# Causal attention stage: turns written out, normed tiles transposed in place, V's bias moved into one output row

## The chip, the cores and the metric

The kernel runs on one core of one Trainium2 chip. Its five engines (TensorE, shown as PE, with its weight loads as PEld; VectorE, DVE; ScalarE, ACT; GpSimd, POOL; SyncE, SP) run their own instruction streams and meet at semaphores. The metric is device time in microseconds (us) for one execution, the median of several; the profile is of one further execution.

## The reference

Two adaLN layers over x of 16 sequences of 256 tokens and 128 channels. Layer 0 has a scan mixer and a six-deep local-attention transformer, layer 1 a causal multi-query attention, then a Mamba block, then a mixture of experts. The change is in the multi-query attention of layer 1:

```python
qkv = x @ wqkv + bqkv
q = qkv[..., :DIM].reshape(b, l, HEADS, HD)       # 16 heads of 8
k = qkv[..., DIM:DIM + HD]                        # one key and one value head for all
v = qkv[..., DIM + HD:]
scores = jnp.einsum('blhd,bmd->bhlm', q, k) / np.sqrt(HD)
scores = jnp.where(causal, scores, jnp.finfo(scores.dtype).min)
attn = jax.nn.softmax(scores, axis=-1)
out = jnp.einsum('bhlm,bmd->blhd', attn, v).reshape(b, l, DIM)
return out @ w_attn_out + b_attn_out
```

Each row of `attn` sums to 1, so a bias b on V adds b to every head's output, and `tile(b, 16) @ w_attn_out` to every row of the result.

## The kernel before

`build` runs the stages one after another, each in a block that ends with a barrier: opening, transformer (six layers), `between_stage` (gate, residual, layer norm into `y`), `mqa_stage` (the stage of the change), mamba, gate, between, mixture of experts, store. In `mqa_stage` the argument `h` is `y`, which lies in SBUF as 32 tiles of 128 tokens; a sequence (a unit) is two tiles.

Work is a software pipeline over 16 units in 19 turns. In turn n, unit n has its front made (transposes L1646, products with Wq L1651 and Wk L1654), unit n-1 its scores (mask L1675, q times k L1681) and at the turn's end its values (`values`, L1657 to L1666), unit n-2 its turned scores (L1700) and first products with V (L1716), unit n-3 the rest and its output (L1737, L1738). `body` of each engine is the order written by hand, and there is no planner. `all_turns` (L1537) writes turns 0 to 3 and 16 to 18 out, with whole numbers for the unit, and runs turns 4 to 15 in a hardware loop of three rounds of four turns, where the semaphore values that are waited for come out of registers. So turn 3 is a written-out turn with all four parts in it, turns 4 to 15 are looped ones, and turn 16 is written out and lacks a front.

`values` fills V for a unit: for each of two tiles a product hT times Wv (32 columns, of which 8 are V) and a second product of a row of ones with `bv`, which adds V's bias and puts the 1 into column 8 (the softmax denominator's column). ScalarE copies both tiles (L1811) into the ring `V1`. On PE what stands behind is the mask of the next unit's first scores, which waits for `maxed`, that is for VectorE's last maximum (L1859) of the turn; the four values steps and that wait are the last thing of a turn on PE.

The transposes at L1646 read `hu`, a double buffer in SBUF that SyncE fills by DMA from `y` (`load`, L1598 to L1600), since a looped turn has no constant address into `y`. The output is added into `y` by VectorE (L1883), three turns later than the front of the same unit.

A matmul of float32 operands shows as two MATMUL records, and one transpose as one.

Of the kernel before, what the change touches and what calls it, by code (L numbers as in the profile page):

```python
# [10 lines left out]
ALU = mybir.AluOpType  # L11
ACT = mybir.ActivationFunctionType
# [4 lines left out]
P = 128  # L17
B = 16
T = 256
TT = T // P  # L20
# [4 lines left out]
class Kernel:  # L25
# [5 lines left out]
    def sb(self, ctx, name, shape, dt=F32):  # L31
        return ctx.enter_context(self.nc.sbuf_tensor(name, shape, dt))
# [5 lines left out]
def sems(nc, ctx, names):  # L38
    return [ctx.enter_context(nc.semaphore(n)) for n in names.split()]
# [1460 lines left out]
QH, QD = 16, 8  # L1500
QG, QS = 4, 4
MQ_ROUNDS = B // 4


def pairs_of_units(engine, body):

    with engine.Fori(0, B // 2 - 1) as i:
        body(i * 2, 0, True)
        body(i * 2 + 1, 1, True)
    body(B - 2, 0, True)  # L1510
    body(B - 1, 1, False)


def tile_of(h, u, t):

    if isinstance(u, int):
        return h[:, u * TT + t, :]
    return h[:, bass.ds(u * TT + t, 1), :].rearrange("p a c -> p (a c)")


class Turn:
# [11 lines left out]
    def has(self, lag):  # L1533
        return not isinstance(self.I, int) or 0 <= self.unit(lag) < B


def all_turns(engine, body):  # L1537
    for k in range(4):
        body(Turn(0, k))
    with engine.Fori(1, MQ_ROUNDS) as I:  # L1540
        for k in range(4):
            body(Turn(I, k))
    for k in range(3):
        body(Turn(MQ_ROUNDS, k))


def mqa_stage(k, h):

    nc, d = k.nc, k.dram
    SCORED = [(0, 0, 0, 4), (0, 1, 0, 4), (1, 0, 0, 2), (1, 1, 0, 2), (1, 0, 2, 2), (1, 1, 2, 2)]
    TURNED = [(0, 0, 0), (0, 0, 1), (1, 0, 0), (1, 0, 1), (1, 1, 0), (1, 1, 1)]
    with ExitStack() as ctx:
        sb = lambda name, shape, dt=F32: k.sb(ctx, "mq_" + name, shape, dt)
        Wq, Wk, Wv, Wout = sb("Wq", [P, QS, P]), sb("Wk", [P, P]), sb("Wv", [P, 32]), sb("Wout", [P, P])
        bq, bk = sb("bq", [P, QS]), sb("bk", [P, 1])
        bv, bout, ones = sb("bv", [1, 32]), sb("bout", [1, P]), sb("ones", [1, P])
        mask32 = sb("mask32", [P, 1, P])
        mask = sb("mask", [P, 1, P], BF16)  # L1560
        identb = sb("identb", [P, P], BF16)
        scratch = sb("scratch", [P, 1])
        hu = sb("hu", [P, 2, TT, P])
        hT = sb("hT", [P, 2, T])
# [3 lines left out]
        V1 = sb("V1", [P, 4, TT, 32])  # L1568
# [9 lines left out]
        ev = lambda name, n=1: Event(nc, ctx, "mq_" + name, n)  # L1578
        loaded, inited, masked = sems(nc, ctx, "mq_loaded mq_inited mq_masked")
        hu_ready = [ev("hu_ready0", 16), ev("hu_ready1", 16)]  # L1580
        f_filled, f_copied = ev("f_filled", 4), ev("f_copied", 4)
# [7 lines left out]
        @block.sync  # L1589
        def _(sp):  # L1590
            for e in hu_ready:
                e.start(sp)
            for dst, name in ((Wq[:, :, :], "mqa_Wq"), (Wk[:, :], "mqa_Wk"), (Wv[:, :], "mqa_Wv"),
                              (Wout[:, :], "L1_attn_w_attn_out"), (bq[:, :], "mqa_bq"), (bk[:, :], "mqa_bk"),
                              (bv[:, :], "mqa_bv"), (bout[:, :], "mqa_bout"), (mask32[:, :, :], "causal_mask")):
                sp.dma_start(dst, d[name]).then_inc(loaded, 16)

            def load(u, p):  # L1598
                sp.wait_ge(f_filled.sem, f_filled.at(u - 2, 1))
                sp.dma_start(hu[:, p, :, :], h[:, bass.ds(u * TT, TT), :]).then_inc(hu_ready[p].sem, 16)  # L1600

            with sp.Fori(0, B // 2) as i:
                load(i * 2, 0)
                load(i * 2 + 1, 1)

        @block.gpsimd
        def _(pool):
            nc.gpsimd.memset(mx[:, :, :, :], 0.0).then_inc(inited, 1)
            nc.gpsimd.memset(ones[:, :], 1.0).then_inc(inited, 1)
            kept.start(pool)  # L1610
            settled.start(pool)
            pool.wait_ge(loaded, 144)

            def keep(n, i, j):
                u, (t, block_, pair) = n.unit(2), TURNED[i]
                pool.wait_ge(settled.sem, settled.at(u, j))
                pool.wait_ge(exped.sem, exped.at(u, i + 1))
                nc.gpsimd.tensor_tensor(scratch[:, :], k.ident[:, 0:1], k.ident[:, 0:1], ALU.mult).then_inc(settled.sem, 1)
                heads = PT[:, i // 2, 2 * pair:2 * pair + 2, :].rearrange("p g (s c) -> p (g s) c", c=P)
                nc.gpsimd.affine_select(heads, heads, pattern=[[0, 2 * QS], [1, P]], base=0, channel_multiplier=-1,  # L1620
                                        compare_op=ALU.is_ge, fill=0.0).then_inc(kept.sem, 1)

            def body(n):
                if n.has(2):
                    keep(n, 0, 0)
                    keep(n, 1, 1)
                    keep(n, 4, 2)
                    keep(n, 5, 3)

            all_turns(pool, body)  # L1630

        @block.tensor
        def _(pe):
            for e in (f_filled, v_filled, scored, x_filled, e_filled, pv_done, back, o_turned, y_done):
                e.start(pe)
            pe.wait_ge(loaded, 144)
            pe.wait_ge(inited, 2)
            pe.wait_ge(masked, 2)

            def front(n, part):  # L1640
                u, p = n.unit(0), n.ring(0, 2)
                if part == 0:
                    pe.wait_ge(hu_ready[p].sem, hu_ready[p].at(n.I * 2 + n.k // 2, 16))
                    pe.wait_ge(v_copied.sem, v_copied.at(u - 2, 1))
                    for t in range(TT):
                        last = nc.tensor.transpose(front_ps[:, t * P:(t + 1) * P], hu[:, p, t, :], k.ident[:, :])  # L1646
                else:
                    pe.wait_ge(f_copied.sem, f_copied.at(u, part))
                    if part < 3:
                        for j in range(2):  # L1650
                            last = nc.tensor.matmul(front_ps[:, j * T:(j + 1) * T], Wq[:, 2 * part - 2 + j, :], hT[:, p, :],  # L1651
                                                    start=True, stop=True)
                    else:
                        last = nc.tensor.matmul(front_ps[:, 0:T], Wk[:, :], hT[:, p, :], start=True, stop=True)  # L1654
                last.then_inc(f_filled.sem, 1)

            def values(n):  # L1657
                u, p = n.unit(1), n.ring(1, 2)
                pe.wait_ge(v_copied.sem, v_copied.at(u - 1, 1))
                if n.has(0):  # L1660
                    pe.wait_ge(f_copied.sem, f_copied.at(n.unit(0), 4))
                for t in range(TT):
                    at = slice(t * 32, (t + 1) * 32)
                    nc.tensor.matmul(front_ps[:, at], hT[:, p, t * P:(t + 1) * P], Wv[:, :], start=True, stop=False)
                    last = nc.tensor.matmul(front_ps[:, at], ones[:, :], bv[:, :], start=False, stop=True)
                last.then_inc(v_filled.sem, 1)  # L1666
# [67 lines left out]
            def output(n, t):  # L1734
                u = n.unit(3)
                pe.wait_ge(oT_ready.sem, oT_ready.at(u, t + 1))
                nc.tensor.matmul(back_ps[:, P:2 * P], oT[:, t, :], Wout[:, :], start=True, stop=False)  # L1737
                nc.tensor.matmul(back_ps[:, P:2 * P], ones[:, :], bout[:, :], start=False, stop=True).then_inc(y_done.sem, 1)  # L1738

# [30 lines left out]

            all_turns(pe, body)

        @block.scalar
        def _(act):
            for e in (f_copied, v_copied, exped, ot_copied, oT_ready):
                e.start(act)
            act.wait_ge(loaded, 144)

            def exponential(n, i):
# [6 lines left out]
            def front(n, part):  # L1786
# [13 lines left out]
                else:  # L1800
                    if not isinstance(u, int) or u >= 4:
                        act.wait_ge(e_filled.sem, e_filled.at(u - 4, 6))
# [3 lines left out]
            def values(n):  # L1806
                u = n.unit(1)
                act.wait_ge(v_filled.sem, v_filled.at(u, 1))
                if not isinstance(u, int) or u >= 4:
                    act.wait_ge(pv_done.sem, pv_done.at(u - 4, 3))  # L1810
                nc.scalar.activation(V1[:, n.ring(1, 4), :, :], front_ps[:, 0:TT * 32].rearrange("p (t e) -> p t e", t=TT),  # L1811
                                     ACT.Copy).then_inc(v_copied.sem, 1)
# [29 lines left out]

            all_turns(act, body)

        @block.vector
        def _(dve):
# [33 lines left out]
            def add_output(n, t):  # L1880
                u = n.unit(3)
                dve.wait_ge(y_done.sem, y_done.at(u, t + 1))
                nc.vector.tensor_tensor(tile_of(h, u, t), tile_of(h, u, t), back_ps[:, P:2 * P], ALU.add)\  # L1883
                    .then_inc(y_added.sem, 1)
# [17 lines left out]

            all_turns(dve, body)

# [350 lines left out]


NE, MR, NS, MS = 16, P // 4, 2, P // 2
HID = NE * MR + NS * MS
# [345 lines left out]
```

## Time and profile before

| | us |
|---|---|
| median of 3 runs | 5036.1 (5034.69 to 5037.89) |
| the profiled execution | 5033.68 |
| its span | 5031.5 |
| multi-query attention in it | 3668.5 to about 4154 |

The page gives each engine's busy time over the span and then its share in 40 slices. The stage lies in slices 30 to 33 counted from 1. PE busy counts the modelled ends of pipelined matmuls, so full PE says that PE was never without a matmul in flight. "issue" as a releaser says that no semaphore held the engine. The mark PEclk is the granted share of TensorE's clock, 1.00 for 2.4 GHz and 0.50 for 1.2 GHz.

### The profile page before, as it was taken

What the parts mean: (1) busy time and instruction counts of PE and PEld (TensorE: products, weight loads), DVE (VectorE), ACT (ScalarE), POOL (GpSimd) and SP (SyncE); (2) the same over time, 40 slices, a digit from 0 to 9 for tenths busy, and PEclk for the clock granted to TensorE, in tenths of its full rate; (3) what the DMA queues carried; (4) which work ended last, traced back from release to release, by engine and by line L of the source; (5) the groups of instructions that cost most, each with busy time, mean ns of one, the idle gap of its engine ahead of it and who ended that gap; (6) DMA issues with size and microseconds to landing.
All of it is one profiled execution on the core that took longest, in us unless ns stands there. A gap on an engine that the chain in (4) does not pass through costs nothing. (4 is left out here: it accounts for less than half of the span.)

```text
span 5031.5 us, 167186 instructions
## 1 busy us (share of the span) xinstructions
PE 4556.1 (91%) x73156; PEld 2966.4 (59%) x73156; DVE 3206.1 (64%) x4495; ACT 2803.1 (56%) x4080; POOL 2573.5 (51%) x1408
## 2 busy tenths in 40 slices
PE   7499999999999999999999999999679998999465
PEld 5266666666666666666666666666445544555244
DVE  3476766767666767667666767677333326888554
ACT  4256665656665656666565656666433435666355
POOL 0266666666666666666666666666221114666400
PEclk8699999999999999999999999999879978999799
DMA  1100001000110010000100011000100002111100
GB/s 53 49 13 18 20 16 37 24 17 20 30 27 20 17 30 24 23 20 17 38 21 18 20 28 32 18 17 19 37 12 5 5 0 76 69 68 69 46 8 21
DMA packets 192843, 138.23 MB, mean 27 GB/s; under 512 B 122572, under 2 KB 178901, under 8 KB 190053
## 3 DMA queue, kind: packets, MB, share of 16 engines
q1 hardware_dynamic: 192101, 127.32, 8.5%
q8 instruction: 590, 9.67, 0.8%
q14 instruction: 152, 1.25, 0.1%
HBM read 68.37 MB, written 4.29 MB: 14 GB/s over the span
## 5 line engine op out<-in xcount | busy, mean ns | idle before, releaser
L1017 POOL TENSOR_TENSOR tf_qk<-tf_qk,tf_rot 128x1024 f32<-128x1024 f32 x384 | 908.7, 2366 | 1217.7 <-DVE tf_rot L1400 1217.7
L1083 PE MATMUL tf_psum<-tf_Wqkv,tf_xsT 128*128 128x512 f32 x1536 | 749.6, 611 | 68.2 <-issue 44.5
L1024 POOL TENSOR_TENSOR tf_qk<-tf_qk,tf_rn 128x1024 f32<-128x1024 f32 x384 | 724.3, 1913 | 54.3 <-ACT tf_rn L1283 54.2
L1276 ACT ACTIVATE tf_sq<-tf_psum 128x1024 f32<-128x1024 f32 x384 | 393.3, 1024 | 533.8 <-DVE tf_rot L1400 533.8
L1396 DVE TENSOR_TENSOR tf_qk<-tf_psum,tf_table 128x1024 f32<-128x1024 f32 x384 | 467.5, 1218 | 265.9 <-PE tf_psum L1083 264.8
L1156 PE MATMUL tf_psum<-tf_probT,tf_V 32*64 32x64 f32 (+1 forms) x27648 | 493.8, 219 | 8.6 <-issue 8.1
L1083 PEld LDWEIGHTS tf_psum<-tf_Wqkv,tf_xsT 128*128 128x128 f32 x1536 | 274.5, 194 | 352.4 <-issue 341.6
L1406 DVE TENSOR_REDUCE tf_ss<-tf_sq 128x16 f32<-128x1024 f32 x384 | 457.6, 1192 | 21.6 <-ACT tf_sq L1276 21.6
L1156 PEld LDWEIGHTS tf_psum<-tf_probT,tf_V 32*64 32x64 f32 x27648 | 442.8, 133 | 47.5 <-issue 42.6
L1400 DVE TENSOR_TENSOR tf_rot<-tf_psum,tf_table 128x1024 f32<-128x1024 f32 x384 | 465.9, 1213 | 0.0
L1065 PE MATMUL tf_psum<-ident,tf_qk 128*128 128x128 f32 x3072 | 408.9, 276 | 3.4 <-ACT tf_qT L1295 2.4
L1065 PEld LDWEIGHTS tf_psum<-ident,tf_qk 128*128 128x128 f32 x3072 | 343.7, 141 | 102.7 <-issue 82.1
L2013 POOL TENSOR_TENSOR mb_read<-mb_state,mb_Csb 128x1024 f32<-128x1024 f32 x128 | 301.6, 2356 | 175.1 <-DVE mb_state L2233 160.0
L1459 DVE SCALAR_TENSOR_TENSOR tf_hT<-tf_psum,tf_b,tf_gel 128x512 f32<-128x512 f32 x144 | 107.5, 746 | 438.4 <-ACT tf_gel L1328 438.4
L1179 PE MATMUL tf_psum<-tf_Wo,tf_oT 128*128 128x128 f32 x3072 | 376.3, 275 | 6.7 <-issue 3.7
L1179 PEld LDWEIGHTS tf_psum<-tf_Wo,tf_oT 128*128 128x128 f32 x3072 | 362.3, 192 | 31.9 <-issue 21.4
L1032 POOL TENSOR_TENSOR tf_prob<-tf_prob,tf_rden 128x1024 f32<-128x1024 f32 x192 | 367.2, 1912 | 13.6 <-DVE tf_rden L1430 13.6
L1099 PE MATMUL tf_psum<-tf_Wqkv,tf_xsT 128*32 128x512 f32 x3072 | 369.5, 598 | 0.0
L1295 ACT ACTIVATE tf_qT<-tf_psum 128x1024 f32<-128x1024 f32 x192 | 196.4, 1023 | 279.0 <-PE tf_psum L1065 278.9
L1124 PEld LDWEIGHTS tf_psum<-tf_kT,tf_qT 64*32 64x32 f32 x24576 | 260.6, 105 | 107.8 <-issue 107.5
L2181 ACT ACTIVATE mb_psum<-mb_delta,mb_A 128x255 f32<-128x255 f32 x512 | 213.4, 462 | 188.3 <-DVE mb_state L2233 185.8
L1124 PE MATMUL tf_psum<-tf_kT,tf_qT 64*32 64x64 f32 x24576 | 295.8, 226 | 21.0 <-issue 21.0
(288 smaller groups left out, 7907.2 us busy)
## 6 DMA issues: line engine op xcount, KB each, us to landing
mb_Csb<-mb_kept SPq DMA_DIRECT2D x16, 2048.0 KB, 7.0
tf_zr<-z SPq DMA_DIRECT2D x96, 128.0 KB, 2.7
z<-tf_z SPq DMA_DIRECT2D x48, 256.0 KB, 2.5
tf_Wqkv<-in_Wqkv_split SPq DMA_DIRECT2D x18, 512.0 KB, 3.7
tf_zu<-z SPq DMA_DIRECT2D x97, 64.0 KB
tf_zu<-z SPq DMA_DIRECT2D x97, 63.5 KB
tf_zsh<-tf_z SPq DMA_DIRECT2D x96, 64.0 KB
tf_zsh<-tf_z SPq DMA_DIRECT2D x96, 63.5 KB
```

Of the source, the lines that this page charges most:

```text
L1017: nc.gpsimd.tensor_tensor(v, v, rot[:, kind, :], ALU.add).then_inc(added.sem, 1)
L1024: nc.gpsimd.tensor_tensor(v, v, rn[:, t, HEADS * kind:HEADS * (kind + 1)].unsqueeze(2) .to_broadcast([P, HEADS, HD]), ALU.mult).then_inc(n ...
L1065: last = nc.tensor.transpose(flat2(trans)[:, j * P:(j + 1) * P], source(j), k.ident[:, :])
L1083: last = nc.tensor.matmul(proj[:, half, :], xsT[:, step.unit(0), WIN + t * P:WIN + (t + 1) * P], Wqkv[:, c:c + 512], start=True, stop=True)
L1099: last = nc.tensor.matmul(score[r:r + 32, m, :], xsT[:, step.unit(2), x:x + WIN], Wqkv[:, c:c + 512], start=True, stop=True)
L1124: last = nc.tensor.matmul(score[w * WIN:(w + 1) * WIN, odd, pair * HD:(pair + 1) * HD], qT[r, t, pair, w * WIN:(w + 1) * WIN], keys, start ...
L1156: last = nc.tensor.matmul(mixed[64 * half:64 * half + 64, odd, j * P + lo:j * P + hi], V[r, step.v_slot(3 + back), v // 2, pair, :], probT ...
L1179: last = nc.tensor.matmul(mixed[:, 0, 0:P], oT[:, t, pair, :], Wo[:, pair, :], start=(pair == 0), stop=(pair == PAIRS - 1))
L1276: nc.scalar.activation(sq[:, kind, :], flat2(proj), ACT.Square).then_inc(squared.sem, 1)
L1396: nc.vector.tensor_tensor(qk[:, t, kind, :].rearrange("p (h e) -> p h e", e=HD), v, cos, ALU.mult)
L1400: nc.vector.tensor_tensor(rot[:, kind, :].rearrange("p (h a e) -> p h a e", a=2, e=HD // 2), swapped, sin, ALU.mult).then_inc(roped.sem, 1)
L1406: nc.vector.tensor_reduce(ss[:, t, HEADS * kind:HEADS * (kind + 1), 0], sq[:, kind, :].rearrange("p (h e) -> p h e", e=HD), AX.X, ALU.add)\
```

## The change

Five edits, all in `mqa_stage` and its helpers:

1. `all_turns` calls `body` for turns 0 to 18 one after another on PE, ACT, DVE and POOL. There is no loop, and all semaphore values and addresses are constants.
2. The buffer `hu`, its two semaphores and SyncE's 16 DMAs are gone. The transposes read the tile in `y`.
3. `values` is one product of 8 columns for each tile, with no bias product. ScalarE copies 8 columns of each tile. V's ring is set to 0 once by POOL, and column 8 to 1.
4. `bv` is V's bias for all 16 heads as a column of 128; before its turns PE computes `bv @ Wout + bout` (one row), ScalarE copies it into `row`, and `row` takes the place of `bout` in `output`.
5. PE and ACT wait for four memsets of POOL in place of two, and PE's very first output waits for `row`.

```diff
-def all_turns(engine, body):
-    for k in range(4):
-        body(Turn(0, k))
-    with engine.Fori(1, MQ_ROUNDS) as I:
-        for k in range(4):
-            body(Turn(I, k))
-    for k in range(3):
-        body(Turn(MQ_ROUNDS, k))
+def all_turns(body):
+    for turn in range(B + 3):
+        body(Turn(turn // 4, turn % 4))
...
-            def load(u, p):
-                sp.wait_ge(f_filled.sem, f_filled.at(u - 2, 1))
-                sp.dma_start(hu[:, p, :, :], h[:, bass.ds(u * TT, TT), :]).then_inc(hu_ready[p].sem, 16)
-
-            with sp.Fori(0, B // 2) as i:
-                load(i * 2, 0)
-                load(i * 2 + 1, 1)
...
+            nc.gpsimd.memset(V1[:, :, :, :], 0.0).then_inc(inited, 1)
+            pool.wait_ge(inited, 3)
+            nc.gpsimd.memset(V1[:, :, :, QD:QD + 1], 1.0).then_inc(inited, 1)
...
-                    pe.wait_ge(hu_ready[p].sem, hu_ready[p].at(n.I * 2 + n.k // 2, 16))
                     pe.wait_ge(v_copied.sem, v_copied.at(u - 2, 1))
                     for t in range(TT):
-                        last = nc.tensor.transpose(front_ps[:, t * P:(t + 1) * P], hu[:, p, t, :], k.ident[:, :])
+                        last = nc.tensor.transpose(front_ps[:, t * P:(t + 1) * P], h[:, u * TT + t, :], k.ident[:, :])
...
                 for t in range(TT):
-                    at = slice(t * 32, (t + 1) * 32)
-                    nc.tensor.matmul(front_ps[:, at], hT[:, p, t * P:(t + 1) * P], Wv[:, :], start=True, stop=False)
-                    last = nc.tensor.matmul(front_ps[:, at], ones[:, :], bv[:, :], start=False, stop=True)
+                    last = nc.tensor.matmul(front_ps[:, t * QD:(t + 1) * QD], hT[:, p, t * P:(t + 1) * P], Wv[:, :],
+                                            start=True, stop=True)
...
+                if u == 0 and t == 0:
+                    pe.wait_ge(row_ready, 1)
...
-                nc.tensor.matmul(back_ps[:, P:2 * P], ones[:, :], bout[:, :], start=False, stop=True).then_inc(y_done.sem, 1)
+                nc.tensor.matmul(back_ps[:, P:2 * P], ones[:, :], row[:, :], start=False, stop=True).then_inc(y_done.sem, 1)
+
+            nc.tensor.matmul(back_ps[0:1, 0:P], bv[:, 0:1], Wout[:, :], start=True, stop=False)
+            nc.tensor.matmul(back_ps[0:1, 0:P], ones[:, 0:1], bout[:, :], start=False, stop=True).then_inc(row_done, 1)
...
+            act.wait_ge(inited, 4)
+            act.wait_ge(row_done, 1)
+            nc.scalar.activation(row[:, :], back_ps[0:1, 0:P], ACT.Copy).then_inc(row_ready, 1)
...
-                nc.scalar.activation(V1[:, n.ring(1, 4), :, :], front_ps[:, 0:TT * 32].rearrange("p (t e) -> p t e", t=TT),
+                nc.scalar.activation(V1[:, n.ring(1, 4), :, 0:QD], front_ps[:, 0:TT * QD].rearrange("p (t e) -> p t e", t=TT),
```

On PE, the end of a looped turn and the start of the next, before (the values step, L1664 and L1665, stands between the last turned scores and the next unit's mask; a REGISTER_ALU row computes a semaphore value and waits for it):

```order
L1700 MATMUL mq_psum<-mq_qa,mq_kT 128x512 [waits mq_exped]
L1700 MATMUL mq_psum<-mq_qa,mq_kT 128x512
L1731 MATMUL mq_psum<-ident,mq_o 128x128 [waits mq_o_ready]
L1661 REGISTER_ALU [waits mq_v_copied]
L1664 MATMUL mq_psum<-mq_Wv,mq_hT 128x32 [waits mq_f_copied]
L1665 MATMUL mq_psum<-mq_bv,mq_ones 128x32
L1664 MATMUL mq_psum<-mq_Wv,mq_hT 128x32
L1665 MATMUL mq_psum<-mq_bv,mq_ones 128x32
L1672 REGISTER_ALU [waits mq_f_copied]
L1675 MATMUL mq_psum<-mq_mask,mq_identb 128x512 [waits mq_maxed]
```

The same place of the changed kernel, on PE:

```order
L1669 MATMUL mq_psum<-mq_qa,mq_kT 128x512 [waits mq_exped,mq_qa_ready]
L1669 MATMUL mq_psum<-mq_qa,mq_kT 128x512
L1700 MATMUL mq_psum<-ident,mq_o 128x128 [waits mq_o_ready]
L1633 MATMUL mq_psum<-mq_Wv,mq_hT 128x8 [waits mq_f_copied,mq_v_copied]
L1633 MATMUL mq_psum<-mq_Wv,mq_hT 128x8
L1644 MATMUL mq_psum<-mq_mask,mq_identb 128x512 [waits mq_maxed,mq_f_copied]
```

Two of the four products are gone, the other two have 8 columns, and the register rows are gone; the neighbours are as they were.

On PE, the stage's start, before:

```order
L1632 UNCONDITIONAL_BRANCH [waits barrier_Pool_Activation_PE_DVE_SP_release]
L1646 MATMUL mq_psum<-ident,mq_hu 128x128 [waits mq_hu_ready0,mq_masked,mq_v_copied,mq_inited,mq_loaded]
L1646 MATMUL mq_psum<-ident,mq_hu 128x128
L1651 MATMUL mq_psum<-mq_hT,mq_Wq 128x256 [waits mq_f_copied]
L1651 MATMUL mq_psum<-mq_hT,mq_Wq 128x256
```

The same place of the changed kernel:

```order
L1603 UNCONDITIONAL_BRANCH [waits barrier_Pool_Activation_PE_DVE_SP_release]
L1711 MATMUL mq_psum<-mq_Wout,mq_bv 1x128 [waits mq_masked,mq_inited,mq_loaded]
L1712 MATMUL mq_psum<-mq_bout,mq_ones 1x128
L1616 MATMUL mq_psum<-ident,y 128x128 [waits mq_v_copied]
L1616 MATMUL mq_psum<-ident,y 128x128
L1621 MATMUL mq_psum<-mq_hT,mq_Wq 128x256 [waits mq_f_copied]
```

The two products of the output row stand ahead of the first transposes, which no longer wait for `hu_ready0`.

## Rows read from the trace of the kernel before

**Rows 1.** The page, parts 1 and 2: busy time, slices of PE and clock

```profile
PE 4556.1 (91%) x73156; PEld 2966.4 (59%) x73156; DVE 3206.1 (64%) x4495; ACT 2803.1 (56%) x4080; POOL 2573.5 (51%) x1408
...
PE   7499999999999999999999999999679998999465
...
PEclk8699999999999999999999999999879978999799
```

**Rows 2.** Stretches: us; busy us of PE, PEld, DVE, ACT, POOL; clock, DMA

```profile
3735.03:3760.55 25.52, 25.52 (x171) 13.62 (x171) 10.02 (x15) 10.23 (x18) 4.92 (x8) 1.00 0.02 6
3760.55:3786.07 25.52, 25.52 (x171) 13.62 (x171) 10.03 (x15) 10.32 (x18) 4.93 (x8) 1.00 0.02 6
...
3862.64:3899.17 36.53, 36.53 (x171) 18.31 (x171) 10.04 (x15) 10.32 (x18) 4.92 (x8) 0.67 0.01 4
3899.17:3926.28 27.11, 27.11 (x171) 14.03 (x171) 10.02 (x15) 10.32 (x18) 4.92 (x8) 0.94 0.01 5
3977.33:4002.86 25.53, 25.53 (x172) 13.63 (x172) 10.04 (x15) 10.33 (x18) 4.92 (x8) 1.00 0.02 5
...
4053.90:4090.43 36.53, 36.53 (x172) 18.41 (x172) 10.03 (x15) 10.32 (x18) 4.92 (x8) 0.67 0.00 0
4090.43:4115.11 24.68, 24.68 (x159) 12.17 (x159) 10.02 (x15) 7.88 (x12) 4.92 (x8) 0.93 0.00 1
```

**Rows 3.** Timeline, end of a looped turn: start, us, engine, line

```profile
3836.21 1.23 DVE L1859 TENSOR_REDUCE mq_mx<-mq_psum 128x4 f32<-128x1024 f32 x1 [2.25 <-PE mq_psum L1681]
...
3837.12 0.31 PE L1664 MATMUL mq_psum<-mq_Wv,mq_hT 128*128 128x32 f32 x2
3837.36 0.40 PE L1665 MATMUL mq_psum<-mq_bv,mq_ones 1*128 1x32 f32 x2
3837.69 0.41 PE L1664 MATMUL mq_psum<-mq_Wv,mq_hT 128*128 128x32 f32 x2
3838.03 0.40 PE L1665 MATMUL mq_psum<-mq_bv,mq_ones 1*128 1x32 f32 x2
3838.36 0.60 PE L1675 MATMUL mq_psum<-mq_mask,mq_identb 128*128 128x512 bf16 x2
```

**Rows 4.** Timeline, the first values step and the last one

```profile
3704.77 1.23 DVE L1859 TENSOR_REDUCE mq_mx<-mq_psum 128x4 f32<-128x1024 f32 x1 [1.56 <-PE mq_psum L1681]
...
3706.12 0.13 PEld L1675 LDWEIGHTS mq_psum<-mq_mask,mq_identb 128*128 128x128 bf16 x2 [0.16 <-issue]
...
4117.52 0.20 PEld L1716 LDWEIGHTS mq_psum<-mq_PT,mq_V 128*32 128x32 f32 x8 [0.75 <-POOL mq_PT L1620]
```

**Rows 5.** Stretches from a values step to the fall of the clock, and behind it

```profile
3704.79:3707.69 2.90, 2.82 (x26) 2.14 (x26) 1.21 (x1) 0.22 (x1) 0.00 (x0) 1.00 0.02 6
3707.69:3724.76 17.07, 17.07 (x66) 7.92 (x62) 4.87 (x5) 4.18 (x6) 2.52 (x4) 0.50 0.02 8
3862.64:3864.70 2.06, 2.06 (x15) 1.47 (x16) 0.32 (x1) 1.37 (x3) 1.00 (x2) 1.00 0.00 0
3864.70:3888.59 23.89, 23.89 (x95) 11.31 (x93) 5.62 (x8) 4.95 (x8) 2.69 (x5) 0.50 0.02 5
3899.17:3902.25 3.08, 3.08 (x29) 2.37 (x29) 0.41 (x2) 1.37 (x3) 1.23 (x2) 1.00 0.00 0
...
4053.90:4055.85 1.95, 1.95 (x13) 1.36 (x14) 0.32 (x1) 1.37 (x3) 0.89 (x2) 1.00 0.00 0
...
4090.43:4093.39 2.96, 2.96 (x28) 2.25 (x28) 0.31 (x1) 1.36 (x3) 1.23 (x2) 1.00 0.00 0
...
4115.11:4117.29 2.18, 1.90 (x13) 1.50 (x12) 0.56 (x2) 1.37 (x3) 1.06 (x2) 1.00 0.00 0
```

**Rows 6.** Timeline, the stage's start, and one output step with half the clock

```profile
3674.01 0.22 DVE L1851 CAST mq_identb<-ident 128x128 bf16<-128x128 f32 x1
...
3675.01 0.66 PE L1646 MATMUL mq_psum<-ident,mq_hu 128*128 128x128 f32 x2 [50.93 <-DMA mq_hu<-y]
...
4151.83 0.79 PE L1738 MATMUL mq_psum<-mq_bout,mq_ones 1*128 1x128 f32 x2
```

More of the change, by code:

```diff
@@ L1502 @@
 MQ_ROUNDS = B // 4
[L1505 to L1518, printed above, removed]
 class Turn:
@@ L1533, in has @@
     def has(self, lag):
-        return not isinstance(self.I, int) or 0 <= self.unit(lag) < B
-def all_turns(engine, body):
-    for k in range(4):
-        body(Turn(0, k))
-    with engine.Fori(1, MQ_ROUNDS) as I:
-        for k in range(4):
-            body(Turn(I, k))
-    for k in range(3):
-        body(Turn(MQ_ROUNDS, k))
+        return 0 <= self.unit(lag) < B
+def all_turns(body):
+    for turn in range(B + 3):
+        body(Turn(turn // 4, turn % 4))
 def mqa_stage(k, h):
@@ L1555, in mqa_stage @@
         sb = lambda name, shape, dt=F32: k.sb(ctx, "mq_" + name, shape, dt)
-        Wq, Wk, Wv, Wout = sb("Wq", [P, QS, P]), sb("Wk", [P, P]), sb("Wv", [P, 32]), sb("Wout", [P, P])
+        Wq, Wk, Wv, Wout = sb("Wq", [P, QS, P]), sb("Wk", [P, P]), sb("Wv", [P, QD]), sb("Wout", [P, P])
         bq, bk = sb("bq", [P, QS]), sb("bk", [P, 1])
-        bv, bout, ones = sb("bv", [1, 32]), sb("bout", [1, P]), sb("ones", [1, P])
+        bv, bout, ones, row = sb("bv", [P, 1]), sb("bout", [1, P]), sb("ones", [1, P]), sb("row", [1, P])
         mask32 = sb("mask32", [P, 1, P])
@@ L1562, in mqa_stage @@
         scratch = sb("scratch", [P, 1])
-        hu = sb("hu", [P, 2, TT, P])
         hT = sb("hT", [P, 2, T])
@@ L1578, in mqa_stage @@
         ev = lambda name, n=1: Event(nc, ctx, "mq_" + name, n)
-        loaded, inited, masked = sems(nc, ctx, "mq_loaded mq_inited mq_masked")
-        hu_ready = [ev("hu_ready0", 16), ev("hu_ready1", 16)]
+        loaded, inited, masked, row_done, row_ready = sems(nc, ctx, "mq_loaded mq_inited mq_masked mq_row_done mq_row_ready")
         f_filled, f_copied = ev("f_filled", 4), ev("f_copied", 4)
@@ L1590, in _ @@
         def _(sp):
-            for e in hu_ready:
-                e.start(sp)
             for dst, name in ((Wq[:, :, :], "mqa_Wq"), (Wk[:, :], "mqa_Wk"), (Wv[:, :], "mqa_Wv"),
@@ L1628, in body @@
                     keep(n, 5, 3)
-            all_turns(pool, body)
+            all_turns(body)
         @block.tensor
@@ L1636, in _ @@
             pe.wait_ge(loaded, 144)
-            pe.wait_ge(inited, 2)
+            pe.wait_ge(inited, 4)
             pe.wait_ge(masked, 2)
@@ L1769, in body @@
                         attend(n, 2, i // 2 - 1)
-            all_turns(pe, body)
+            all_turns(body)
         @block.scalar
@@ L1800, in front @@
                 else:
-                    if not isinstance(u, int) or u >= 4:
+                    if u >= 4:
                         act.wait_ge(e_filled.sem, e_filled.at(u - 4, 6))
@@ L1808, in values @@
                 act.wait_ge(v_filled.sem, v_filled.at(u, 1))
-                if not isinstance(u, int) or u >= 4:
+                if u >= 4:
                     act.wait_ge(pv_done.sem, pv_done.at(u - 4, 3))
-                nc.scalar.activation(V1[:, n.ring(1, 4), :, :], front_ps[:, 0:TT * 32].rearrange("p (t e) -> p t e", t=TT),
+                nc.scalar.activation(V1[:, n.ring(1, 4), :, 0:QD], front_ps[:, 0:TT * QD].rearrange("p (t e) -> p t e", t=TT),
                                      ACT.Copy).then_inc(v_copied.sem, 1)
@@ L1841, in body @@
                         values(n)
-            all_turns(act, body)
+            all_turns(body)
         @block.vector
@@ L1882, in add_output @@
                 dve.wait_ge(y_done.sem, y_done.at(u, t + 1))
-                nc.vector.tensor_tensor(tile_of(h, u, t), tile_of(h, u, t), back_ps[:, P:2 * P], ALU.add)\
+                nc.vector.tensor_tensor(h[:, u * TT + t, :], h[:, u * TT + t, :], back_ps[:, P:2 * P], ALU.add)\
                     .then_inc(y_added.sem, 1)
@@ L1901, in body @@
                         normalise(n, 2, 0)
-            all_turns(dve, body)
+            all_turns(body)
 DI, DS, DC, DR = 2 * P, 16, 4, P // 16
@@ L2254, in _, with pairs_of_units, tile_of @@
                     add_output(s // PAIRS - 1)
+def pairs_of_units(engine, body):
+    with engine.Fori(0, B // 2 - 1) as i:
+        body(i * 2, 0, True)
+        body(i * 2 + 1, 1, True)
+    body(B - 2, 0, True)
+    body(B - 1, 1, False)
+def tile_of(h, u, t):
+    if isinstance(u, int):
+        return h[:, u * TT + t, :]
+    return h[:, bass.ds(u * TT + t, 1), :].rearrange("p a c -> p (a c)")
 NE, MR, NS, MS = 16, P // 4, 2, P // 2
@@ L2579 @@
     one = (np.arange(32) == QD).astype(np.float32)
-    arrays.update(mqa_Wq=group(w[:, :P]), mqa_Wk=rows(w[:, P:P + QD]), mqa_Wv=np.pad(w[:, P + QD:], ((0, 0), (0, 32 - QD))),
+    arrays.update(mqa_Wq=group(w[:, :P]), mqa_Wk=rows(w[:, P:P + QD]), mqa_Wv=w[:, P + QD:],
                   mqa_bq=group(bias[None, :P])[0].T, mqa_bk=(rows(bias[None, P:P + QD])[0] + np.tile(one, QG))[:, None],
-                  mqa_bv=np.pad(bias[None, P + QD:], ((0, 0), (0, 32 - QD))) + one,
+                  mqa_bv=np.tile(bias[P + QD:], QH)[:, None],
                   mqa_bout=a["L1_attn_b_attn_out"][None, :], L1_attn_w_attn_out=a["L1_attn_w_attn_out"])
```

## The prediction

> **What bounds the kernel now.** First the page: PE is busy 91% of the span, the other engines between 51% and 64%, and in the slices of this stage (30 to 33 of 40) PE stands at 7 and three times at 9, while the clock's digit goes 7, 9, 9, 7 [rows 1]. Next the stage cut at its values steps, which gives one turn per row [rows 2]. Fourteen such stretches run from 3735.03 to 4115.11. In each, PE is busy for the whole stretch, while VectorE and ScalarE work 10 us of it and GpSimd 4.9 us. Ten of them, at a clock of 1.00, last 25.52 or 25.53 us; four are shown, the other six read alike. Such sameness to 0.01 us says that PE's own work paces the stage: no wait ends last in it. Two stretches last 36.53 us with a clock of 0.67, one 27.11 us with 0.94, and the last, 24.68 us, has no front in it and a clock of 0.93. So there are two ways to be faster here: less work on PE, or a clock that falls less.
>
> **The loop (edit 1).** The trace has its own comparison. The stretch from 3735.03 lies in turn 3, which is written out in the kernel before too; the one from 3760.55 is turn 4, the loop's entry and first pass; the one from 3977.33 is turn 12, with a branch back at its start. They last 25.52, 25.52 and 25.53 us [rows 2]. Register rows and branches are done while PE's queue still holds matmuls. I cost the loop's removal at 0. Its bounds are the 0.01 us by which these rows differ, 0.2 us over 16 turns, either way. The cover is PE's full queue; where PE drains at the ends of the stage the turns were written out already. The Trainium skill, page Runtime: NRT & Kernel Launch, section Instruction fetch mechanics, speaks for a gain: a taken branch to a target outside the fetched pages stalls until a DMA brings it. By that rule the stretch with the branch back should be longer than the written-out one; by the row it is not, and the sum would gain nothing from it that these rows could hide.
>
> **The copies through hu (edit 2).** SyncE's DMAs are issued two turns ahead, and in the stretches above PE has no idle time that they could end [rows 2]. Only the first is waited for: PE's first transposes start at 3675.01, released by that DMA, while the cast of the identity, the last of the other things that it waits for, ends at 3674.23 [rows 6]. Without it they could start about 0.75 us sooner. The transposes of a tile read y three turns before VectorE adds into it, so no new wait comes in.
>
> **The output row (edits 4 and 5).** Two products, four MATMUL records, now stand there. The nearest row is the product with bout at half the clock: a pair lasts 0.79 us with its tail [rows 6]; two pairs behind one another 1.2 us, taken with one tail. Net of the 0.75 us the start is 0.45 us later; bounds 0 and 0.9. ScalarE's copy of the row ends before the transposes do and hides behind them. PE asks for the row only in turn 3, some 60 us later. GpSimd's two further memsets run beside the loads of the weights. Waits on them: 0.
>
> **The values step (edit 3).** It takes from 3837.12 to 3838.36, 1.24 us, and starts of its four products are 0.33 us apart, whether the product has 128 rows or one [rows 3]. Two of four go: 0.67 us per turn. The two that stay go from 32 columns to 8. Since the one-row product costs as much as the other, what they cost is mostly loads of 128 columns, which stay; I count nothing for the narrower ones (bounds 0, and 0.5 us a turn if the 0.67 us left went with the columns). What could take the gap over: the mask behind it waits for VectorE's maximum, which ends at 3836.21 + 1.23 = 3837.44; the mask would start at 3838.36 - 0.67 = 3837.69. So 0.25 us of cover is left, enough, and a gain beyond it would be cut off there. In the first values step, turn 1, that cover is missing: the maximum ends at 3706.00 and the mask starts at 3706.12, so it gains 0.1 us. Behind the last one, turn 16, PE waits 0.75 us for GpSimd at 4117.52 anyway, so it gains 0 [rows 4]. Fourteen turns are left: 14 x 0.67 = 9.4, with turn 1 9.5 us. Less the start's 0.45, **9.0 us** of work gone. ScalarE's narrower copy is off the path.
>
> **The clock.** What did PE do before each fall? There are six in the stage from its first values step to its last, at 3707.69, 3864.70, 3902.25, 4055.85, 4093.39 and 4117.29. Counted back to the start of the nearest values step they come 2.90, 2.06, 3.08, 1.95, 2.96 and 2.18 us behind it [rows 5]. Never does the clock fall in the other 20-odd us of a turn, though PE is just as "busy" there. The values step is the turn's thinnest stretch: in 1.24 us eight records stream 32 columns each, and four of these use one row of the array, while other steps stream 128 to 512 columns. The other ten values steps have no fall behind them, so it also takes a certain alignment. What the falls cost: the turns with one are 36.53 - 25.52 = 11.01 us longer, twice, and the short second fall that follows each costs 27.11 - 25.52 = 1.59 us; the one inside the 24.68 us stretch is of the same length (a mean clock of 0.93 means that 24.68 x 0.07 / 0.5 = 3.5 us ran at 0.50, and 0.94 over 27.11 us gives 3.3), so I take 1.59 again. Together 25.2 us of the stage. The change halves that thin stretch to about 0.6 us, and dense work (masks, scores, turned scores) closes in from both sides, so that the thinnest place of the turn is clearly less thin. I expect the four falls in the middle, those at 3864.70, 3902.25, 4055.85 and 4093.39, not to come: **25.2 us**. The falls behind turn 1 and turn 16 I let stand, as the removed work leaves a wait there [rows 4].
>
> **Sum.** Against the profiled execution: 5033.68 - 9.0 - 25.2 = 4999.5 us. The median of the runs shown is 2.4 us above that execution, so 5036.1 - 34.2 = 5001.9, rounded to **5002 us**.
>
> **Rivals.** (B) The falls stay as they are, two pairs: only the 9.0 us go, 5027.1 us. For it: PE shows full in the rows ahead of each fall [rows 5], so "busy" gives no hint that less work would help. The Trainium skill, TensorE: Matmul & The Clock Gate, section HAM oscillation, lays falls to idle gaps of PE; by that rule removing busy work changes none of them, and this rival holds, but the rows show falls with no gap and always behind the same step. (C) One of the two pairs stays, as the shorter turn now meets the bad alignment elsewhere: 5036.1 - 9.0 - 12.6 = 5014.5 us. (A+) The falls behind turn 1 or turn 16 go too. The one at 3707.69 lasts 17.07 us [rows 5], at the middle ones' price (11.01 us for 23.89) 7.9 us: 4994 us. (D) The other side: the shorter turn meets the clock more often, not less. The place is the same thin step; each further pair of falls costs 12.6 us. One more gives 5036.1 - 9.0 + 12.6 = 5039.7, two more 5052.3 us. It decides at the second extra pair, and needs the halved step to be as harmful as the whole one. Against it: ten whole steps of sixteen are harmless now. (E) The edit does less than it says: VectorE's maximum or the extra fetch of written-out code takes the 0.67 us. With the falls gone anyway 5011 us, with them 5036. Against it: 0.25 us of cover, and no idle time in turn 3.
>
> **Chances.** A 0.58, A+ 0.08, C 0.13, B 0.14, E 0.04, D 0.03. A measurement of this kernel can tell about 0.2%, 10 us, from no change; the line is at 5026.0. A, A+, C and half of E are faster by more; a fifth of B's width (narrower products, up to 0.25 us more per turn, 3.5 us) lies beyond the line too. Faster 0.83, within 0.13, slower 0.04. The range reaches from below A+ with its bounds, 4990, to B with the start's bound, 5028; it leaves out D and the ends of A+.
>
> **What would show it.** Stretches from values step to values step all at 24.85 us with a clock of 1.00, no 36.5 us one between turn 2 and turn 15: A. Stretches at 24.85 us with one or two long ones: C or B. Stretches still at 25.5 us with VectorE or "issue" ahead of the mask: E. Idle time of PE with no semaphore behind it in the middle of the stage would mean that written-out code is not fetched in time. First transposes at 3675.5 and not at 3675.0 confirm the start's term. It would be wrong if falls came behind another step of the turn, which no row now shows.

## The result, and the profile after

The changed kernel took 4999.93 us, the median of 7 runs from 4994.37 to 5018.81; the kernel before, beside it, 5036.51 us. The ratio is 0.9936 with a 95% interval of 0.9918 to 0.9955. Forecast were 5002 us and a gain of 34.2; measured is a gain of 36.6 us. A second set of 6 runs gave 4997.6 us and 0.9932 (0.9909 to 0.9955).

The profiled execution happens to be a long one, 5018.34 us with a span of 5016.3, so its total says little and its stretches are what to read. Its page, parts 1 and 2:

```profile
PE 4546.4 (91%) x73096; PEld 2960.5 (59%) x73096; DVE 3206.0 (64%) x4495; ACT 2800.8 (56%) x4081; POOL 2573.8 (51%) x1410
...
PE   7499999999999999999999999999769989999466
...
PEclk8699999999999999999999999999859989999788
```

Against [rows 1] PE is busy 9.7 us less and its weight loads 5.9 us less, PE's share of the span is the same 91%, and no other engine's time moved by more than 2.3 us. That the 9.7 us lie near the forecast's 9.0 us of work is chance: busy time also grows and shrinks with the clock. From these totals nobody could say where the gain comes from. The Trainium skill, page Trainium Kernel Development and Optimization, section Performance Expectations, calls matmul busy time a bad measure of how near a kernel is to roofline (the most that the engine can do). The two profiles agree with that: 91% before and 91% after.

The stage cut again at its values steps (the changed kernel; stretch, us, busy us of PE, PEld, DVE, ACT, POOL, then the clock and DMA). The first row is from the stage's start to the values step of turn 2, the last from the last values step to the stage's end:

```profile
3669.70:3748.41 78.71, 66.42 (x254) 34.97 (x254) 17.09 (x19) 13.70 (x27) 5.20 (x10) 0.53 0.03 7
3748.41:3773.15 24.74, 24.74 (x168) 12.98 (x168) 10.03 (x15) 10.09 (x18) 4.92 (x8) 1.00 0.00 1
3896.81:3921.55 24.74, 24.74 (x168) 12.98 (x168) 10.03 (x15) 10.09 (x18) 4.92 (x8) 1.00 0.00 1
4069.95:4092.26 22.31, 22.31 (x155) 11.03 (x155) 10.02 (x15) 7.74 (x12) 4.92 (x8) 1.00 0.00 1
4092.26:4129.70 37.44, 29.39 (x96) 10.75 (x95) 3.52 (x11) 9.76 (x15) 6.15 (x10) 0.58 0.00 0
...
3748.41:4069.95 321.54, 321.54 (x2160) 168.67 (x2160) 130.32 (x183) 131.10 (x222) 64.06 (x104) 1.00 0.00 1
```

These answer to [rows 2]. The last row holds the thirteen stretches of the middle in one: 321.54 us, 24.73 each, at a clock of 1.00 throughout. Before, the same thirteen took from 3735.03 to 4090.43, 355.40 us. With the fourteenth (24.68 before, 22.31 now) the middle went from 380.1 to 343.85 us, 36.2 us less. Of that, the work is about 14 x 0.79 = 11.1 us, and the falls of the clock are the other 25.2 us.

The values step itself (changed kernel, timeline, end of a turn):

```profile
3895.91 1.23 DVE L1836 TENSOR_REDUCE mq_mx<-mq_psum 128x4 f32<-128x1024 f32 x1 [2.25 <-PE mq_psum L1650]
...
3896.81 0.51 PE L1633 MATMUL mq_psum<-mq_Wv,mq_hT 128*128 128x8 f32 x4
3897.28 0.59 PE L1644 MATMUL mq_psum<-mq_mask,mq_identb 128*128 128x512 bf16 x2
```

It takes 0.47 us to the next mask, where [rows 3] had 1.24. VectorE's maximum ends at 3897.14, 0.14 us before the mask: of the 0.25 us of cover that the prediction counted, 0.14 is left. In turn 16 no mask stands behind the step, and there the two products take 0.38 us up to the next instruction:

```profile
4092.26 0.51 PE L1633 MATMUL mq_psum<-mq_Wv,mq_hT 128*128 128x8 f32 x4
4092.64 0.66 PE L1660 MATMUL mq_psum<-ident,mq_mx 128*128 128x128 f32 x4
```

### The profile page after: what moved, and what is told of

Same layout as the page of the kernel before. It is cut to its first block and busy times, and to the rows that moved or that the text cites. A ratio compares the mean times of both kernels' runs of the same rounds, so it can differ in the third digit from the quotient of the medians.

```text
span 5016.3 us, 166479 instructions
## 1 busy us (share of the span) xinstructions
PE 4546.4 (91%) x73096; PEld 2960.5 (59%) x73096; DVE 3206.0 (64%) x4495; ACT 2800.8 (56%) x4081; POOL 2573.8 (51%) x1410
```

## Experiments

The theory (1): the clock falls where PE's turn is thinnest, at the values step, and a shorter step ends that. Rivals: the written-out turns steadied the stage (2); only the amount of work counts (3). A "thin" stretch is one in which PE streams few columns for each load of weights, or uses few rows of its array. Each diff shows the lines that matter; the buffers, memsets and waits that go with them are left out.

### Edits 3 and 4 alone

The kernel before with the 8-column products, no bias product and the output row; loops and copies stay.

```diff
                 for t in range(TT):
-                    at = slice(t * 32, (t + 1) * 32)
-                    nc.tensor.matmul(front_ps[:, at], hT[:, p, t * P:(t + 1) * P], Wv[:, :], start=True, stop=False)
-                    last = nc.tensor.matmul(front_ps[:, at], ones[:, :], bv[:, :], start=False, stop=True)
+                    last = nc.tensor.matmul(front_ps[:, t * QD:(t + 1) * QD], hT[:, p, t * P:(t + 1) * P], Wv[:, :],
+                                            start=True, stop=True)
```

> Edits 3 and 4 alone (V's bias out, 8 columns, output row); the loops and the copies through hu stay. Theory 1 (the clock falls behind the thin values step, and the shorter step ends that): all of the gain is here, 5000 us, 0.993 of before; the middle turns between values steps last 24.75 us with a clock of 1.00, and no stretch of 36.5 us stands between turns 2 and 15. Theory 2 (written-out turns are what steadied the clock or the time): only the removed products show, 5025 us, 0.998, with two stretches of about 36 us left.

Measured: 5003.2 us, 0.9938 (0.9921 to 0.9954). Stretches of this kernel, columns as above; the last row holds twelve looped turns:

```profile
3729.30:3754.03 24.73, 24.73 (x167) 12.97 (x167) 10.02 (x15) 10.09 (x18) 4.93 (x8) 1.00 0.02 7
3754.03:3778.69 24.66, 24.66 (x168) 12.92 (x167) 10.03 (x15) 10.19 (x18) 4.93 (x8) 1.00 0.02 6
...
3754.03:4049.93 295.90, 295.90 (x1993) 154.99 (x1993) 120.33 (x169) 122.09 (x205) 59.13 (x96) 1.00 0.01 5
```

The whole gain is here. The first row is turn 3, written out in this kernel too: 24.73 us, as in the changed kernel. A looped turn is 0.07 to 0.08 us shorter. So loops cost nothing here, and writing them out costs 12 x 24.73 - 295.90 = 0.9 us, too little to see in the total.

### Edits 1 and 2 alone

The changed kernel with the values step of the kernel before and without the output row.

```diff
-                    last = nc.tensor.matmul(front_ps[:, t * QD:(t + 1) * QD], hT[:, p, t * P:(t + 1) * P], Wv[:, :],
-                                            start=True, stop=True)
+                    at = slice(t * 32, (t + 1) * 32)
+                    nc.tensor.matmul(front_ps[:, at], hT[:, p, t * P:(t + 1) * P], Wv[:, :], start=True, stop=False)
+                    last = nc.tensor.matmul(front_ps[:, at], ones[:, :], bv[:, :], start=False, stop=True)
```

> Edits 1 and 2 alone (turns written out, tiles transposed in y); the bias products stay in the values step. Theory 1: no gain beyond the first transposes' 0.75 us, 5036 us, 1.000 of before; turns of 25.52 us, and two stretches of about 36.5 us with half the clock in part of each. Theory 2: the falls in the middle are gone, 5011 us, 0.995.

Measured: 5035.44 us, 0.9995 (0.9985 to 1.0006), over 10 runs; the profiled execution, 5053.87 us, is the longest of them. Stretches of this kernel, the second and the fourth being the half clock inside the one before:

```profile
3735.52:3761.04 25.52, 25.52 (x171) 13.62 (x171) 10.02 (x15) 10.23 (x18) 4.92 (x8) 1.00 0.01 1
...
3761.04:3797.57 36.53, 36.53 (x172) 18.29 (x172) 10.03 (x15) 10.32 (x18) 4.92 (x8) 0.67 0.00 0
3763.12:3787.02 23.90, 23.90 (x95) 11.25 (x91) 5.61 (x8) 4.95 (x8) 2.73 (x5) 0.50 0.00 1
...
3952.29:3988.82 36.53, 36.53 (x171) 18.39 (x171) 10.03 (x15) 10.32 (x18) 4.92 (x8) 0.67 0.00 0
3954.26:3978.16 23.90, 23.90 (x95) 11.47 (x93) 5.61 (x8) 4.95 (x8) 2.85 (x5) 0.50 0.00 1
```

Written-out turns of 25.52 us, and the long falls again 2.1 and 2.0 us behind the start of a values step. In this execution there are three pairs of a long and a short fall in the middle, not two (the third begins at 4041.45), so how many there are varies with the execution. Theory 2 falls.

### The thin work moved

The changed kernel with two one-row products of 32 columns in the output steps; `zeros` is a row of zeros.

```diff
                 nc.tensor.matmul(back_ps[:, P:2 * P], oT[:, t, :], Wout[:, :], start=True, stop=False)
+                nc.tensor.matmul(back_ps[:, P:P + 32], ones[:, :], zeros[:, :], start=False, stop=False)
```

> The changed kernel with two one-row products of 32 columns (they add a row of zeros) put into the two output steps of each turn, so PE has as many product instructions as before, but none of them in the values step. Theory 1 (it is the place of the thin work): turns of 25.4 us, no fall of the clock in the middle turns, so the changed kernel's time plus 14 x 0.67 = 9.4: 5009 us, 0.995 of before. Rival (it is the sum of thin work in a turn): the falls are back, two stretches of 36 us, 5034 us, 0.9995.

Measured: 5001.9 us, 0.9942 (0.9923 to 0.9961). Its thirteen middle stretches in one:

```profile
3740.41:4064.89 324.48, 324.48 (x2212) 174.30 (x2212) 130.35 (x183) 131.18 (x222) 64.05 (x104) 1.00 0.00 1
```

24.96 us a turn, no fall: where the thin products stand decides, not how many there are. The price was wrong. The two cost 0.23 us a turn here, not 0.67. One of them costs all of it, and the other nothing. From the product with `Wout` to the next mask it is 0.83 us in the changed kernel and 1.06 here; in the other output step, which has turned scores behind it, the second pair of turned-score records starts 0.96 us behind the product with `Wout` in the changed kernel and 0.97 here. The rows are of this kernel, first the step ahead of a mask, then the other:

```profile
3894.88 0.49 PE L1709 MATMUL mq_psum<-mq_Wout,mq_oT 128*128 128x128 f32 x2
3895.94 0.60 PE L1645 MATMUL mq_psum<-mq_mask,mq_identb 128*128 128x512 bf16 x2
...
3881.05 0.49 PE L1709 MATMUL mq_psum<-mq_Wout,mq_oT 128*128 128x128 f32 x2
3882.02 0.59 PE L1670 MATMUL mq_psum<-mq_qa,mq_kT 32*128 32x512 f32 x2
```

### The thin step longer

The kernel before with two more one-row products in the values step.

```diff
                     nc.tensor.matmul(front_ps[:, at], hT[:, p, t * P:(t + 1) * P], Wv[:, :], start=True, stop=False)
+                    nc.tensor.matmul(front_ps[:, at], ones[:, :], zeros[:, :], start=False, stop=False)
                     last = nc.tensor.matmul(front_ps[:, at], ones[:, :], bv[:, :], start=False, stop=True)
```

> The kernel before with two more one-row products of 32 columns (they add zeros) in the values step, which so takes about 1.9 us in place of 1.24. Theory 1: each turn gets 0.67 us longer, and the clock falls behind far more of the values steps, in every turn or every second one, at 11 to 13 us each: 5036 + 9.4 + 50 to 100, some 5115 us, 1.016 of before. Rival (the falls have nothing to do with the length of that step): 5036 + 9.4 = 5045 us, 1.002, still two stretches of 36 us.

Measured: 5069.26 us, 1.0077 (1.0049 to 1.0106), from 5061.96 to 5097.85; the profiled execution is the longest of them. Its stretches:

```profile
3779.58:3807.12 27.54, 27.54 (x176) 14.74 (x176) 10.04 (x15) 10.32 (x18) 4.92 (x8) 0.94 0.02 6
3782.37:3785.78 3.41, 3.41 (x24) 1.65 (x20) 1.82 (x2) 0.00 (x0) 0.00 (x0) 0.50 0.00 0
3807.12:3844.05 36.93, 36.93 (x175) 18.68 (x175) 10.02 (x15) 10.32 (x18) 4.92 (x8) 0.68 0.01 4
3809.68:3833.58 23.90, 23.90 (x96) 11.21 (x93) 5.61 (x8) 4.95 (x8) 2.46 (x4) 0.50 0.02 5
3844.05:3871.55 27.50, 27.50 (x175) 14.53 (x175) 10.02 (x15) 10.31 (x18) 4.92 (x8) 0.94 0.02 6
...
3779.58:4138.14 358.56, 358.56 (x2089) 187.67 (x2089) 120.32 (x169) 123.81 (x205) 59.09 (x96) 0.86 0.01 4
```

The last row holds twelve turns, and in every one the clock fell: in nine for 3.4 us (27.5 us a turn), in three for 23.9 us (36.9 us a turn). The direction and the count are the theory's, the amount is not: most falls were short ones, at some 1.6 us each, where I had priced 11 to 13. So the total is 33 us over the kernel before, where some 80 were forecast. The two more products were cheaper too: the step takes 1.69 us, 0.45 more than before, not 0.67 more.

```profile
3844.05 0.31 PE L1665 MATMUL mq_psum<-mq_Wv,mq_hT 128*128 128x32 f32 x2
...
3845.74 0.60 PE L1677 MATMUL mq_psum<-mq_mask,mq_identb 128*128 128x512 bf16 x2
```

### More work beside the thin step

The kernel before, nothing taken away, and three dense products ahead of the values step, into columns of the bank that nobody reads.

```diff
+                for _ in range(3):
+                    nc.tensor.matmul(front_ps[:, P:4 * P].rearrange("p (s c) -> p s c", s=3), identb[:, :],
+                                     mask[:, 0:1, :].to_broadcast([P, 3, P]), start=True, stop=True)
                 for t in range(TT):
                     at = slice(t * 32, (t + 1) * 32)
```

> The kernel before with more work: ahead of each values step three dense products of 384 columns (identity times mask, into columns that nobody reads). Each costs 0.16 us of streaming at the full clock, 0.48 us a turn. Theory 1 (the clock falls where the turn is thinnest, and dense work beside the thin step ends that): turns of about 26.0 us, no fall in the middle, so 5036 + 14 x 0.48 - 25 = 5018 us, 0.9965 of before, though nothing was taken away. Rival (only less work in the values step helps): 5036 + 7 = 5043 us, 1.0013, with two stretches of 37 us or more.

Measured: 5008.45 us, 0.9944 (0.9923 to 0.9964). Its thirteen middle stretches in one, and its stage's start up to the values step of turn 2:

```profile
3728.85:4067.03 338.18, 338.18 (x2252) 181.58 (x2251) 130.43 (x182) 134.03 (x222) 64.02 (x104) 1.00 0.01 5
3666.50:3728.85 62.35, 50.03 (x259) 28.46 (x260) 17.41 (x19) 13.95 (x26) 4.81 (x8) 0.71 0.07 19
```

26.01 us a turn, 0.49 more than before, and no fall: 338.2 us where the kernel before took 355.4. With more work the kernel is 0.56% faster. That settles theory 1 against 3. It also answers a further rival, that a turn of 25.52 us only happens to meet the clock badly: with the clock full, a turn of the kernel with the longer thin step would last about 25.52 + 0.45 = 25.97 us (an estimate), nearly this kernel's 26.01, and there the clock fell in all twelve turns, here in none. The total is also 10 us better than I expected. In the profiles the stage's start took 62.35 us at a clock of 0.71, where the kernel before took 66.53 at 0.65, and from turn 16's values step to the start of the last addition into `y` it took 32.98 at 0.67, where it was 37.55 at 0.57: 8.8 us together.

### The width of the two products

The changed kernel with Wv of 32 columns, 24 of them zeros.

```diff
-                    last = nc.tensor.matmul(front_ps[:, t * QD:(t + 1) * QD], hT[:, p, t * P:(t + 1) * P], Wv[:, :],
+                    last = nc.tensor.matmul(front_ps[:, t * 32:(t + 1) * 32], hT[:, p, t * P:(t + 1) * P], Wv[:, :],
```

> The changed kernel with Wv of 32 columns again (24 are zeros), still without a bias product. It tells what the narrower products are worth. If the two products are bound by loading 128 columns of weights, as the prediction had it: turns of 24.73 us as in the changed kernel, 5000 us. If the columns count: 25.52 - 0.67 = 24.85 us, the clock as in the changed kernel, 5002 us. No fall in the middle turns by theory 1 either way; if the falls come back, the narrower products and not the two removed ones were what ended them.

Measured: 4997.66 us, 0.9927 (0.9904 to 0.995). Stretches and values step of this kernel:

```profile
3732.15:4053.68 321.53, 321.53 (x2159) 168.70 (x2159) 130.44 (x183) 131.11 (x222) 64.03 (x104) 1.00 0.00 1
...
3831.08 0.53 PE L1633 MATMUL mq_psum<-mq_Wv,mq_hT 128*128 128x32 f32 x4
3831.55 0.59 PE L1644 MATMUL mq_psum<-mq_mask,mq_identb 128*128 128x512 bf16 x2
```

The same 24.73 us and the same 0.47 us step. In turn 16, where no wait for VectorE could hide a difference, the two products of 32 columns take 0.37 us, and the two of 8 columns took 0.38:

```profile
4076.00 0.53 PE L1633 MATMUL mq_psum<-mq_Wv,mq_hT 128*128 128x32 f32 x4
4076.37 0.66 PE L1660 MATMUL mq_psum<-ident,mq_mx 128*128 128x128 f32 x4
```

The narrower products are worth nothing, for the work or for the clock.

### Filler where PE waits

The changed kernel with products that nobody reads, first at the stage's start, then in its last turns too. `fill` issues identity times mask, 512 columns each.

```diff
+            for _ in range(4):
+                nc.tensor.matmul(pv_ps[:, :], k.ident[:, :], k.x[:, 0:4, :], start=True, stop=True)
             pe.wait_ge(loaded, 144)
...
+                if part and u == 0:
+                    fill(pv_ps, 4)
...
+                if u == 0:
+                    fill(pv_ps, 4)
                 if i == 0:
                     pe.wait_ge(f_copied.sem, f_copied.at(u, 4))
...
+                if u == B - 1:
+                    fill(score[:, 0], 3)
                 pe.wait_ge(qa_ready.sem, qa_ready.at(u, t + 1))
```

The first three places:

> The changed kernel with filler on PE: four products of 512 columns while it waits for the stage's weights, and 2048 columns of mask products ahead of each wait of turn 0 and of the scores of unit 0. By theory 1 the clock is full from turn 0 on, and the stage's first 78 us (start to the values step of turn 2), which ran mostly at half clock, get 10 to 25 us shorter: 4985 us, 0.990 of before. Rival: the filler delays as much as the clock gives back, 5000 to 5010 us.

Measured: 4989.37 us, 0.99 (0.9879 to 0.9921). All four:

> As the one before, and three mask products of 512 columns ahead of each turned score of the last unit, where PE waits for ScalarE's exponentials. By theory 1 the last 37 us of the stage lose their half clock and some 6 to 8 us: 4978 us, 0.9885. Rival: waits for ScalarE and GpSimd set the pace there and the clock does not matter: as the one before.

Measured: 4980.33 us, 0.9883 (0.986 to 0.9906). Its median is the lowest here, below both kernels; its interval and that of the kernel with three places overlap. The start and the tail of the first, and the tail of the second:

```profile
3671.40:3725.14 53.74, 50.69 (x298) 26.89 (x298) 17.10 (x19) 13.72 (x27) 5.21 (x10) 0.95 0.04 10
4068.99:4103.50 34.51, 26.47 (x96) 9.64 (x95) 3.52 (x11) 9.77 (x15) 6.17 (x10) 0.65 0.00 0
...
4077.68:4107.80 30.12, 23.55 (x114) 9.39 (x113) 3.52 (x11) 9.77 (x15) 6.15 (x10) 0.92 0.00 1
```

The start took 78.71 us at a clock of 0.53 in the changed kernel's first profile, and 67.09 at 0.65 in its second (below); it takes 53.74 at 0.95. The tail went from 37.44 at 0.58, and 34.51 at 0.65 without its own filler, to 30.12 at 0.92. The filler did not hold in every execution: the second kernel's profiled one, 4990.8 us, has a start of 63.34 us at 0.79.

```profile
3670.50:3733.84 63.34, 60.39 (x298) 31.22 (x299) 17.10 (x19) 13.70 (x27) 5.18 (x10) 0.79 0.04 8
```

The same filler with loops and copies kept:

> Edits 3 and 4 with the loops and the copies through hu kept, and the filler of the fastest kernel so far. If written-out turns are worth nothing, it equals that kernel: 4980 us, 0.9885 of before, with turns of 24.66 us in the loop (as in the run of edits 3 and 4 alone). If writing out helps where the stage is not paced by PE's full queue, it is slower by more than 5 us.

Measured: 4982.35 us, 0.9895 (0.9862 to 0.9929); equal to the one above within the intervals, which are too wide to rule out the 5 us. Its twelve looped turns took 295.90 us, 24.66 each.

### The changed kernel again

> The changed kernel once more, for the spread of its times and a second profile. If the spread comes from how long the clock stays low at the stage's start and elsewhere outside the middle turns, the middle turns are 24.73 us again, and the difference between the two profiled executions lies ahead of the values step of turn 2 and behind the stage; median 5000 us. If falls come back in the middle in some executions, a stretch of 36 us shows.

Measured: 4997.6 us, from 4986.3 to 5016.07. The profiled execution is the shortest, 4986.3 us, 32 us less than the first one. Its start and its fourteen middle stretches:

```profile
3659.00:3726.09 67.09, 54.37 (x254) 29.00 (x255) 17.09 (x19) 13.71 (x27) 5.21 (x10) 0.65 0.03 8
...
3726.09:4069.94 343.85, 343.85 (x2314) 179.72 (x2313) 140.39 (x197) 138.94 (x233) 69.14 (x112) 1.00 0.00 1
```

The middle is the same 343.85 us. The 32 us lie in the stages ahead (the stage starts at 3659.0 in place of 3669.7, 10.7 us), in this start (11.6 us, at a clock of 0.65 in place of 0.53) and behind it (1.5 us in the tail, 7.8 us in the later stages).

## Why the prediction was right

- **What bounds the kernel**: right. PE without a wait paced every middle turn before and after, to 0.01 us.
- **The loop, at 0**: right for the total, but its bounds of 0.2 us were too narrow, and the sign is the opposite of what one would hope: the written-out form costs 0.07 us a turn, 0.9 us in all. It does so in the one place where PE now stands close behind VectorE. Looped (edits 3 and 4 alone), the mask starts at 3877.70, 0.38 us behind the step's start and 0.06 us behind the end of the maximum at 3877.64; written out, 0.47 and 0.14 us behind. Why is not settled.
- **The copies and the output row**: the identity's cast ends at 3675.50, the row's products start at 3675.65 and the transposes at 3676.68, so the row costs 1.03 us where I took 1.2. From SyncE's first issue to the first transposes it is 6.92 us now and was 6.36: 0.56 us later, forecast 0.45.
- **The values step, 0.67 us a turn**: the size was off, 0.79 measured. The step that failed is the 0.33 us from start to start as the price of every product. The starts in [rows 3] are 0.24, 0.33, 0.34 and 0.33 us apart, and two products less left 0.57 us for the other two. They take 0.38 us by themselves and 0.47 with the written-out mask behind them. So a product costs less when no one-row product stands beside it; that it is the one-row product's load that made the difference is my reading and not shown. Their columns do not matter, as forecast. The cover of 0.25 us held and now limits more: a step shorter still would gain at most 0.14 us written out.
- **The clock, 25.2 us**: right, in place, count and size. No fall is left in the middle in any of the eight profiles of kernels with the short step (three of them with filler at the ends), nor with dense work beside the long one; all of the twelve turns of the kernel with a longer one have a fall. The size has luck in it: it was taken from one execution of the kernel before, which had two pairs of falls and lay 2.4 us from the median. The execution of edits 1 and 2 alone that was profiled, with the same values step, had three pairs, which at the same price are 37.8 us.
- **The falls behind turns 1 and 16 stay**: right in both profiles of the changed kernel, but these falls do not bear on the thin step. In the first profile the clock falls at 3709.24, 0.2 us behind the start of turn 1's values step at 3709.04, when that step has hardly begun; in the second it falls 3.2 us behind it. In turn 16 it falls 2.7 and 4.4 us behind, and between the step and the fall PE waits 1.38 us for GpSimd. The prediction's words that PE shows full ahead of each fall hold for the four in the middle only: [rows 5] has 2.82 of 2.90 us and 1.90 of 2.18 us ahead of the first and the last (and the first step starts at 3704.66, not 3704.79, so that fall comes 3.03 us behind it). The first fall also varied from 17.07 to 37.55 us at half the clock, which I had not in the sum.

```profile
3709.04 0.87 PE L1633 MATMUL mq_psum<-mq_Wv,mq_hT 128*128 128x8 f32 x4
...
4094.67 1.71 PE L1685 MATMUL mq_psum<-mq_PT,mq_V 128*32 128x512 f32 x8 [1.38 <-POOL mq_PT L1591]
...
3709.24:3746.79 37.55, 36.93 (x136) 18.12 (x137) 9.02 (x10) 8.32 (x13) 3.75 (x6) 0.50 0.00 1
...
3698.84:3715.91 17.07, 17.07 (x62) 7.81 (x62) 4.87 (x5) 4.19 (x6) 2.52 (x4) 0.50 0.00 0
```

The last row is of the changed kernel's second profile, the others of its first. The length of that fall and the other stages make the 32 us between the two profiles. Its runs spread from 4986 to 5019 us, most likely for the same reasons, but only these two have a profile. A single profile of it misleads: 5018.34 us against the kernel before's 5033.68 would read as a gain of 15.

Rival B rested on PE being busy ahead of each fall, and on the Trainium skill's rule (TensorE: Matmul & The Clock Gate, section HAM oscillation) that idle gaps of PE cause the falls. The measurement decides against it for this stage: PE shows no idle time for 13 turns, and the clock falls or does not by what stands in 1.24 us of them and right beside it. What in the step does it stays open: the short step has fewer products, no one-row product and less time, all at once, and no run has four products of 128 rows in its place.

## What to carry to other kernels

Cut a steady loop at one instruction and compare the pieces with the granted clock beside them; where one piece is 40% longer with the same instructions, look at what PE did in the few microseconds before the clock fell. A step of many tiny products is dearer than its time if it stands alone: shorten it, move its parts between wide products, or put dense work beside it. Writing a loop out was worth nothing here, where PE was never without a matmul in flight.

## What the runs showed that was not expected

- More work made the kernel faster: 0.49 us more per turn on PE, 0.9944 of the time (0.9923 to 0.9964).
- A one-row product has no one price. Taking two out of the values step gave 0.86 us looped (1.24 - 0.38), 0.43 each; adding two more to it cost 0.45, some 0.22 each; in the output steps one cost 0.23 us and one nothing.
- Falls come in two lengths in the middle turns, and these are the same in different kernels: 23.89 us in the kernel before, 23.90 us with edits 1 and 2 alone and with the longer step, and 3.41 us for the short ones. A longer thin step made many short ones and three long ones in twelve turns; the theory does not say which a fall becomes, and no run here settles it.
- Filler at the start and in the tail, where PE waits for other engines, gave a further 20 us over the changed kernel (4980.33 against 4999.93 us), though not in every execution.
